# Mamba and mixture-of-experts layer on one core: the first chunk's diagonals, silus, softplus quarters, loads and first decays in another order

## What is computed

```python
xn = norm(x) * ln_g + ln_b                      # after a first layernorm of x
u, z = split(xn @ W_in.T)
u_c = silu(causal_conv4(u) + conv_b)
dt, Bm, Cm = split(u_c @ W_xp.T)                # 16, 16 and 16 columns
dt = softplus(dt @ W_dt.T + b_dt)
h = exp(dt * A) * h + (dt * u_c) * Bm           # per token, 512 channels x 16 states
y = (h . Cm + u_c * D) * silu(z)
x = x + (x' + y @ W_out.T)                      # then layernorm, router, top 2 of 8 experts
```

## Time and profile before

| | us |
|---|---|
| median of 3 runs | 2284.62 |
| lowest, highest | 2284.24, 2291.43 |
| the profiled execution | 2288.1 |
| its span, first to last instruction | 2285.8 |
| mean granted TensorE clock | 0.899 of 2.4 GHz |

### The profile page before, as it was taken

How to read it: one execution, slowest core, us unless ns; L and a number is a source line. 1 busy time by engine, 2 the same in 40 slices (tenths; PEclk the granted TensorE clock), 3 DMA queues, 4 the chain that set the end, 5 groups by cost and what they waited for, 6 DMA issues and landing times.

```text
span 2285.8 us, 32608 instructions
## 1 busy us (share of the span) xinstructions
PE 1772.3 (78%) x7694; PEld 916.3 (40%) x7694; DVE 1895.2 (83%) x2462; ACT 1807.1 (79%) x3754; POOL 1935.4 (85%) x1190
## 2 busy tenths in 40 slices
PE   5666757597878879687888878787887978766687
PEld 2212313143444435343434435343543534343444
DVE  0389998899988998898998898899898998999622
ACT  5889788888888888988898788888888888773333
POOL 1488898899989998998989898898989999998445
PEclk9788979798989989898999989899999989886899
DMA  1545555477778767777877767677876777697642
GB/s 58 129 103 132 113 125 121 112 170 179 173 174 200 178 170 172 183 175 172 200 178 197 160 179 177 161 175 177 217 168 173 185 181 185 160 236 214 176 94 32
DMA packets 217980, 369.35 MB, mean 162 GB/s; under 512 B 31040, under 2 KB 86592, under 8 KB 217664
## 3 DMA queue, kind: packets, MB, share of 16 engines
q1 hardware_dynamic: 192208, 333.56, 59.4%
q0 software_dynamic: 25584, 33.71, 7.6%
HBM read 285.05 MB, written 83.01 MB: 161 GB/s over the span
## 4 chain that ended last, share of the span: by engine, by line
POOL 23%; issue 23%; PE 20%; ACT 18%; DVE 9%; DMA 5%; POOLq 0%; ACTq 0%; DVEq 0%; SPq 0%
POOL arena L1417 8%; DVE dA L1180 5%; ACT dA L1039 5%; DMA out<-yt,xt 5%; POOL arena L1425 4%; PE ring L650 4%; POOL out L1471 3%; POOL sorted_x L1458 3%; PE ring L658 2%; DVE arena L1180 2%; PE yps L746 2%; POOL arena L1440 1%; POOL arena L1435 1%; PE p_g L778 1%; ACT L972 1%
## 5 line engine op out<-in xcount | busy, mean ns | idle before, releaser
L1417 POOL TENSOR_TENSOR arena<-arena,b_bc 128x2048 f32<-128x2048 f32 x256 | 998.5, 3900 | 79.1 <-PE yps L746 79.0
L1039 ACT ACTIVATE dA<-arena,a_s 128x512 f32<-128x512 f32 x1024 | 680.7, 684 | 116.8 <-DVE arena L1189 71.0
L1180 DVE TENSOR_TENSOR_SCAN dA<-dA,arena 128x512 f32<-128x512 f32 x384 | 454.5, 1214 | 161.0 <-ACT dA L1039 111.6
L1180 DVE TENSOR_TENSOR_SCAN dA<-dA,carry,arena 128x512 f32<-128x512 f32 x384 | 477.5, 1274 | 52.9 <-POOL arena L1417 35.9
L746 PE MATMUL yps<-arena,const_s 128*32 128x512 f32 x2048 | 316.3, 694 | 60.1 <-POOL arena L1425 38.1
L1425 POOL TENSOR_TENSOR arena<-arena,c_bc 128x511 f32<-128x511 f32 (+1 forms) x256 | 335.1, 1309 | 28.9 <-DVE arena L1180 27.2
L1189 DVE TENSOR_TENSOR arena<-dA,c_bc 128x1024 f32<-128x1024 f32 x256 | 313.7, 1225 | 8.8
L642 PE MATMUL ring<-arena 128*128 128x512 f32 x488 | 266.0, 672 | 59.7 <-ACT arena L939 24.5
L778 PEld LDWEIGHTS p_g<-xT,w_e 128*128 128x128 f32 x1680 | 218.4, 210 | 128.5 <-issue 128.5
L650 PE MATMUL ring<-arena 128*128 128x512 f32 x480 | 232.3, 628 | 35.4 <-ACT arena L939 13.7
L778 PE MATMUL p_g<-xT,w_e 128*128 128x128 f32 x1680 | 238.3, 300 | 22.0 <-DVE hT L1329 22.0
(11 more groups left out here) (194 smaller groups left out, 3001.3 us busy)
## 6 DMA issues: line engine op xcount, KB each, us to landing
arena<-dt_d SPq DMA_DIRECT2D x512, 256.0 KB, 6.7
w_e<-in_w_moe SPq DMA_DIRECT2D x105, 512.0 KB, 5.9
dt_d<-arena SPq DMA_DIRECT2D x128, 256.0 KB, 2.4
w_e<-in_w_moe SPq DMA_DIRECT2D x105, 256.0 KB, 7.7
b_bc<-bc_d SPq DMA_DIRECT2D x256, 64.0 KB, 2.3
c_bc<-bc_d SPq DMA_DIRECT2D x256, 64.0 KB, 5.3
xt<-sorted_x SPq DMA_DIRECT2D x120, 129.0 KB, 3.6
xs<-in_x SPq DMA_DIRECT2D x16, 512.0 KB, 4.4
```

The lines of the kernel that those rows point to most:

```text
L1039: act.activation(dA[:, j, :], rep_dt[:, c % 2, j, :], ACT.Exp, scale=a_s[:, n, j:j + 1]).then_inc(s_exp, 1)
L1180: return dve.tensor_tensor_scan(out_ap, dA[:, j, :], hs[:, u % 3, j, :], init, ALU.mult, ALU.add)
L1417: pool.tensor_tensor(hs[:, u % 3], rep_dtu[:, c % 2], b_bc[:, g, :].unsqueeze(1).to_broadcast([P, J, T]), ALU.mult).then_inc(s_dbu, 1)
```

## The change

Only the front of chunk 0, and six items of chunk 1 (X0, X1, U0, U1, W0, W1), are placed anew:

- DVE makes the diagonals, one product of 128x512 per block and one for d_skip, at the start; ACT no longer does, and waits for s_w only before it takes X0. The rates (`decay_rates`) move from slot -17 to -21.
- In chunk 0 each W is followed by its own silu of 128x512 (`first_silu`), and x_proj waits block by block.
- D1's dt_proj and softplus go right behind D0's, D2's to slot -8, D3's to slots 1 and 2; POOL's steps likewise. Chunk 1's X0 and X1 go to slots -7 and -6, U0 to -5, U1 to 0 (made at -4), W0 and W1 to 1 and 2 (made at 0 and 1).
- The four decays of unit 0 stand at slot -5 (before: slot -1, between other items), the drives of units 0, 1 and 2 at slots -5, -4 and -2 (before: each one slot ahead of its unit).
- SP loads b and c of two groups, then after dt's first quarter is stored its repeats (dtu first), then b and c of the other groups.

```diff
-def listed(table, first, last, s, place):
-
+def moved_all(table, places):
+    for name, at in places.items():
+        table = moved(table, name, at)
+    return table
+
+
+def listed(tables, s, place):
+    first, second, table, last = tables
     return [(q, k) for q in range(NQ) for k in
-            (first if q == 0 else table if q < NQ - 1 else last).get((s - UN * q, place), [])]
+            (first if q == 0 else second if q == 1 else table if q < NQ - 1 else last).get((s - UN * q, place), [])]
+
+
+MAKES_FIRST = moved_all(MAKES0, {"D1": (-13, 1), "D2": (-8, 1), "D3": (1, 0)})
+TAKES_FIRST = moved_all(TAKES0, {"D1": (-12, 3), "E1": (-12, 4), "L1": (-10, 2), "D2": (-8, 2), "E2": (-8, 3), "L2": (0, 1),
+                                 "D3": (1, 1), "E3": (1, 2), "L3": (2, 2)})
+MAKES_SECOND = moved_all(MAKES, {"X0": (-23, 1), "X1": (-22, 1), "U0": (-21, 1), "U1": (-20, 1), "W0": (-16, 2), "W1": (-15, 2)})
+TAKES_SECOND = moved_all(TAKES, {"X0": (-23, 2), "X1": (-22, 2), "U0": (-21, 1), "U1": (-16, 1), "W0": (-15, 0), "W1": (-14, 0)})
...
-FIVE = sum(q == 0 and name[0] in "XUWPZ" or name == "D0" and q == 0 for q, name in RING)
+FIVE = sum(q == 0 and name[0] in "XUWPZ" or name in ("D0", "D1") and q == 0 for q, name in RING)
...
+            def first_rep(k, dst, s):
+                sp.wait_ge(s_dtw[0], 32)
+                for r in range(R):
+                    sp.dma_start(dst[32 * r:32 * r + 32, 0], dt_d[0, k, 0].rearrange("(j d) t -> d j t", j=J)).then_inc(s[0], 16)
...
                 if s == -12:
-                    for g in range(G):
+                    for g in range(2):
                         load_b(0, g)
+                        load_c(0, g)
+                if s == -9:
+                    first_rep(1, rep_dtu, s_rdtu)
+                    first_rep(0, rep_dt, s_rdt)
+                    for g in range(2, G):
+                        load_b(0, g)
+                        load_c(0, g)
                 if q == NQ - 1 and n in (4, 5, 6, 7, 9, 10, 13, 14):
                     load_late((4, 5, 6, 7, 9, 10, 13, 14).index(n))
...
-                    pe.wait_ge(s_diag, (TAPS + 1) * (c + 1))
+                    pe.wait_ge(s_diag, c + 1 if c < CC - 1 else CC + 1)
...
-                pe.wait_ge(s_uc, q + 1)
+                if q > 0:
+                    pe.wait_ge(s_uc, CC + q)
                 for c in range(CC):
+                    if q == 0:
+                        pe.wait_ge(s_uc, c + 1)
                     last = pe.matmul(bank(q, "P0")[0:RANK + 2 * NS, :], w_xp_s[:, c, :], uc[:, q % 2, c, :], start=c == 0, stop=c == CC - 1)
...
-            def diagonals(c):
-                for k in range(TAPS):
-                    act.activation(d_conv[:, c, k, :], ident, ACT.Copy, scale=chan_s[:, c, k:k + 1]).then_inc(s_diag, 1)
-                act.activation(d_skip[:, c, :], ident, ACT.Copy, scale=chan_s[:, c, TAPS + 2:TAPS + 3]).then_inc(s_diag, 1)
...
+            def first_silu(c):
+                act.wait_ge(s_ract, TAKEN[0, f"W{c}"])
+                act.activation(uc[:, 0, c, :], uc[:, 0, c, :], ACT.Silu).then_inc(s_uc, 1)
...
-            diagonals(0)
             for s in range(FIRST, TOTAL_SLOTS):
                 q, n = s // UN, s % UN
+                if s == -5:
+                    for j in (0, 1, 3, 2):
+                        decay(0, j)
                 for p in ahead(s, 12, -9):
                     norm_x(p)
...
-                if 0 <= s + 1 < UN * NQ:
+                if 0 <= s < UN * NQ - 1:
                     decay(s + 1, 0)
...
-                if s in (FIRST + 3, FIRST + 4, FIRST + 5):
-                    diagonals(s - FIRST - 2)
-                if s == FIRST + 6:
+                if s == FIRST + 2:
...
+            def diagonals():
+
+                dve.wait_ge(s_w, 80)
+                for c in range(CC):
+                    dve.tensor_tensor(d_conv[:, c], ident.unsqueeze(1).to_broadcast([P, TAPS, P]),
+                                      chan_s[:, c, 0:TAPS].unsqueeze(2).to_broadcast([P, TAPS, P]), ALU.mult).then_inc(s_diag, 1)
+                dve.tensor_tensor(d_skip[:], ident.unsqueeze(1).to_broadcast([P, CC, P]),
+                                  chan_s[:, :, TAPS + 2:TAPS + 3].to_broadcast([P, CC, P]), ALU.mult).then_inc(s_diag, 1)
...
+                if s in (-5, -4, -2):
+                    drive({-5: 0, -4: 1, -2: 2}[s])
+                if 1 < s < UN * NQ - 1:
                     drive(s + 1)
...
-                for p, k in pieces(s, (-8, -3, 0, 2), (-11, -1, 1, 2)):
+                for p, k in pieces(s, (-8, -3, 0, 2), (-11, -9, 0, 3)):
                     less_lost(p, k)
                 if n == 2 and 0 <= q - 1 < NQ:
                     mean(q - 1)
-                for p, k in pieces(s, (-7, -2, 0, 4), (-11, -1, 1, 4)):
+                for p, k in pieces(s, (-7, -2, 0, 4), (-11, -9, 0, 4)):
                     plus_relu(p, k)
-                for p, k in pieces(s, (-9, -4, -1, 1), (-12, -3, 0, 1)):
+                for p, k in pieces(s, (-9, -4, -1, 1), (-12, -10, -3, 2)):
                     round_off(p, k)
-                for p, k in pieces(s, (-6, -2, 0, 4), (-11, -1, 1, 4)):
+                for p, k in pieces(s, (-6, -2, 0, 4), (-11, -9, 0, 4)):
                     dtu(p, k)
```

32 lines of the change are left out of this document (18 added, 14 removed).

## The result

The changed kernel takes 2267.56 us, the median of four executions (2264.78 to 2271.98), against 2285.63 for the kernel before (four executions, 2284.24 to 2291.43). That is 18.1 us less, and the quotient of the two medians is 0.9921. The ratio on record, which isn't that quotient, is 0.9907, with a 95% interval of 0.9888 to 0.9927 that holds both. Forecast were 2269.2 us and 15.4 us less.

What follows compares the result with a forecast made beforehand. No engine is full; the first 92 us are a prologue whose time counts one to one in the total. Gains 3.2 + 5.95 + 5.4 + 0.9 = 15.4 us off the median 2284.62 give 2269.2 us, range 2258 to 2279.

Steps and rivals of the forecast that it cites:

- At par: From unit 4 on: both orders are the same on every engine, so the gain is carried whole to the end.
- Part A: Start to the first norm_x: totals start at 6.0, 4.5 us earlier, less 1.3 for the collision; gain 3.2 us.
- The collision: First deviation: DVE's diagonals and POOL's small steps exclude each other, costing 1.3 us, between 0 and 2.65.
- The bound of 2.65: First deviation, worst case: POOL does nothing until DVE's diagonals end at 12.4, then needs its whole 3.0 us.
- Part B: Convolutions to x_proj's end: silus between convolutions, x_proj at full clock, 9.4 us becomes 3.45; gain 5.95 us.
- Part C: x_proj's end to the first decay: takes, waits and a table load leave, D2 enters, 36.4 becomes 31.0; gain 5.4 us.
- Part D: First four units, now holding U0, U1, W0 and D3: 32.3 us becomes 31.4; gain 0.9 us.
- such a one took 5.44 us: Unit 1: W0's convolution, starting on a PE that stood waiting, takes 5.44 us, so the unit takes 8.95.
- Rival 1: First four units: each 9.2 us, as POOL's fourth drive waits for PE; 5.4 us less gain, 2274.6 us; chance 0.14.
- Rival 2: First chunk's units 5 to 15 wait and give back all 15.4 us; 2284.6 us; chance 0.08.
- Rival 3: Seventh unit of every chunk: PE's clock at 1.2 GHz, +50 - 15.4 us, 2319 us; chance 0.02.
- Rival 4: No collision at the start and kinder clocks in the seventh units, 1.3 + 7 us more; 2261 us; chance 0.12.

Runs made afterwards that it cites:

- delay: The changed kernel plus four ACT copies of unused or later overwritten tiles directly ahead of the first decays; 2275.07 us, ratio 0.9933.
- again: The changed kernel executed once more in a second group, same program with no edit; 2272.58 us, ratio 0.9919.
- dose: The changed kernel with all five DVE diagonals waiting for ACT's squares, so they begin with POOL's deviation steps; 2268.76 us, ratio 0.9916.
- u_diag: The changed kernel with the diagonals back on ACT, which waits for s_w at its start again; 2274.71 us, ratio 0.9935.
- u_silu: The changed kernel with one silu of 2048 elements behind all four convolutions again, x_proj waiting for it; 2275.72 us, ratio 0.9933.
- no_coll: The changed kernel with DVE's second to fifth diagonals waiting until POOL's first deviation is done; 2266.48 us, ratio 0.9895.
- no_coll2: The same program as no_coll, executed once more in the last group; 2265.86 us, ratio 0.9906.
- router: no_coll with the router's matmuls moved from ahead of x_proj to behind it, in all chunks but the last; 2301.72 us, ratio 1.0053.
- u_front: The changed kernel with items, decays, drives, POOL's pieces and SP's order as before; new diagonals and silus stay; 2278.24 us, ratio 0.9959.
- xs_late: The changed kernel with the second half of chunk 1's norm_x on ACT moved from ahead of the first decays to slot 5; 2271.13 us, ratio 0.9908.
- whole: The changed kernel with x_proj waiting for all four silus, which stay by block; 2273.23 us, ratio 0.9931.
- both: The changed kernel with the edits of no_coll and xs_late together; 2275.48 us, ratio 0.9923.

## Why the prediction was right

**What bounds the start.** Right in the main. Time taken from the prologue is time of the total: 14.5 us at the first product became 16.9 at the 17th and 15.6 of the span. "At par" was a little too much: of the 17.5 us at the fifth product 0.6 were gone at the 17th, and of delay's 5.5 us 1.3. The pace behind is kept. The window from chunk 1's first scan to the last product with C in the kernel before:

```profile
212.40:2139.30 1926.90, 1524.38 (x6869) 797.35 (x6870) 1748.87 (x2230) 1591.95 (x3264) 1757.18 (x1060) 0.90 0.72 175
```

Counted from the products themselves, it is 2139.3 - 214.9 = 1924.4 before and 2124.5 - 198.0 = 1926.5 after, 2.1 more; the seventh units alone are 4.0 more. Behind the last product 0.8 us is won.

**Part A, 3.2.** Measured 17.23 - 13.98 = 3.25. The totals start at 6.00 as said. The collision cost 1.1 where 1.3 was taken. The reason given ("two waits of 0.69 at a product's end") was nearly it: there are three waits, 0.44, 0.34 and 0.33, and by the place of the first they can sum to 0.7, as in again. The bound of 2.65, POOL still until DVE ends, can't be reached in this way, since POOL's step slips in at the first end of a product; dose shows that more products don't raise the loss. The Trainium skill, SBUF — State Buffer, section Who interferes with whom, calls the port pair that the two share an exclusive lock, and says that whoever issues first decides who blocks. For a step's start under a DVE product the rows agree. But no row of the deviation shows the other half, a DVE product held by a POOL instruction that began first: the diagonals ran at 0.6 us each under POOL's 2.00 us step. The 3.77 us instance of the earlier trace rows shows that such a hold exists beside a drive, so the kind of POOL's instruction matters, and for this step (8 elements per partition) the measurement decides. Why the two differ no run here shows.

**Part B, 5.95.** Measured: before 17.23 to 55.19, 37.96; after 13.98 to 46.18, 32.20: 5.76. x_proj took 3.63 at the full clock, where 3.44 was put. Again cuts the same time otherwise: 3.65 for part A and 4.99 for part B, so each of them is known to 0.8 us only, and their sum (9.0 and 8.6) to 0.4.

**Part C, 5.4.** Measured: before 55.19 to 91.57, 36.38; after 46.18 to 77.10, 30.92: 5.46. The first decay is 0.1 from its forecast. SP's order was not in the way: the first two drives ran at 68.06 to 75.6 on POOL, forecast to end by 75.5.

**Part D, 0.9.** This term was mis-sized, by 2.1 us, of which unit 1 is 1.35. The units took 6.5, 7.6, 7.4 and 7.8, 29.3 in sum, where 31.4 was put; the gain is 3.0. The fifth product stands at 109.49, not at 111.5. The step that failed is "such a one took 5.44 us": unit 1 was priced with a convolution at the slow clock. PE in the change:

```profile
86.58 3.70 PE L675 MATMUL ring<-arena 128*128 128x512 f32 x8 [0.93 <-ACT arena L961]
```

It ran at the full clock. And that wasn't luck of one execution: with the pause of 0.93 us ahead of it, as here, it took 3.70 in all eight executions of the new order (the change, again, u_diag, u_silu, no_coll, no_coll2, dose, router), and unit 1 took 7.6 to 7.8 in each. The two executions of the old order, before and u_front, have the same pause and 5.44 and 5.36. So the price was read from an order in which the clock was low at this place, and carried over to one in which it isn't; why the same pause goes with either level no run shows. Among the kernels with another pause, only xs_late had the 5.40 and a unit 1 of 8.5; delay, whole and both had 3.70 and 6.8 to 7.2.

**Rival 1.** Its mechanism is there and its price isn't. POOL in the change:

```profile
94.24 3.81 POOL L1458 TENSOR_TENSOR arena<-arena,b_bc 128x2048 f32<-128x2048 f32 x1 [3.29 <-PE yps L774]
```

The fourth drive waits 3.29 us for PE's first product into yps, as the rival had it, and ends at 98.05. DVE scans the fourth unit from 99.29, so 1.2 us were left; the drives stand far enough ahead. **Rival 2** fell by the 17th product, 16.9 us earlier here and in again, and by delay. **Rival 3**: two of 15 seventh units took 14.5 and 14.6 before and two 14.5 after; the sum rose by 4.0, within the 6 us put for it. **Rival 4** fell: the collision is real, and the seventh units were dearer, not cheaper; the 2 us more came from part D.

Span against span the sum is 15.4 forecast and 15.6 measured. That it is so near is partly luck: D gave 2.1 more, which repeats in again, while the seventh units took 4.0 and the rest of chunk 0 another 0.6, with 1.9 and 0.8 won elsewhere behind. Against the medians the gain is 18.1 in one group and 16.6 in the other.

**A better version?** no_coll is the best measured: 2266.48 and 2265.86 us. In the traces it is ahead of the change by 1.0 us at the 17th product. Its medians are 6.1 below again and 2.9 below dose beside it, with intervals of the ratios that overlap in both cases. The spans of the profiled executions of no_coll and again differ by 6.5, of which 5.9 lie in the seventh units (164.8 against 170.7); dose, with the collision, has the same 165.6 as no_coll2 without it. So the collision isn't what the seventh units hang on, and whether the edit is better by more than 1 us stays open.
